# A layer on one core: where the shared expert's gate is applied, and when the expert slots are worked out and filled

## The reference, cut to what matters

```python
logits = x_flat @ gate_w.T                       # 8 experts, 512 tokens
scores = softmax(logits); w = scores * in_top2   # two experts per token
h = silu(g) * u                                  # routed experts, inner width 704
out = einsum('neh,ne->nh', expert_out, w)
shared = silu(x_flat @ shared_gate_w.T) * (x_flat @ shared_up_w.T) @ shared_down_w.T   # inner width 1408
shared_weight = sigmoid(x_flat @ shared_expert_gate_w.T)      # one number per token
out = out + shared_weight * shared
```

## Time and profile before

| | |
|---|---|
| median of three runs | 723.59 us |
| profiled execution, its time / its span | 723.02 / 721.3 us |
| PE busy | 699.9 us, 97% |
| DVE busy | 573.9 us, 80% |
| ACT busy | 336.3 us, 47% |
| POOL busy | 197.3 us, 27% |
| granted TensorE clock, mean | 0.995 |

### The profile page before, as it was taken

The page is one execution under the profiler, slowest core; times in us unless marked ns, Lnnn a source line. Parts: engine busy times, 40 slices in busy tenths (PEclk is TensorE's granted clock), DMA queues, the critical chain, the costliest instruction groups (busy, mean ns, idle before and its releaser), DMA issues.

```text
span 721.3 us, 9895 instructions
## 1 busy us (share of the span) xinstructions
PE 699.9 (97%) x3209; PEld 573.9 (80%) x3209; DVE 573.9 (80%) x714; ACT 336.3 (47%) x449; POOL 197.3 (27%) x143
## 2 busy tenths in 40 slices
PE   7999999999999999999999999899999999999996
PEld 6888888888887788888888888668777888888884
DVE  6477888777979998899994734678677799899896
ACT  4322222222245555656662424632233588887871
POOL 4335445454430000000000001334893111212153
PEclk9999999999999999999999999999999999999997
DMA  8046676776632237232202406122300799999973
GB/s 307 2 159 202 222 231 225 253 226 229 233 123 97 88 117 320 88 113 91 87 29 92 186 0 248 48 84 103 117 3 1 289 343 351 387 386 365 407 276 121
DMA packets 38541, 130.68 MB, mean 181 GB/s; under 512 B 6642, under 2 KB 10484, under 8 KB 35444
## 3 DMA queue, kind: packets, MB, share of 16 engines
q1 hardware_dynamic: 35972, 124.85, 47.8%
q0 software_dynamic: 1536, 4.20, 1.8%
q10 hardware_dynamic: 1008, 1.32, 0.6%
HBM read 120.89 MB, written 9.46 MB: 181 GB/s over the span
## 4 chain that ended last, share of the span: by engine, by line
PE 87%; DVE 9%; issue 2%; ACT 2%; DMA 0%; DVEq 0%; ACTq 0%
PE ps L886 21%; PE ps L853 8%; PE ps L849 8%; PE ps L850 8%; PE ps L1071 5%; PE ps L805 5%; PE ps L807 5%; PE ps L806 5%; PE ps L1041 4%; PE ps L1052 3%; PE ps L1050 3%; PE ps L1051 3%; DVE hid L1476 1%; PE ps L1058 1%; DVE wu_lo L1544 1%
## 5 line engine op out<-in xcount | busy, mean ns | idle before, releaser
L429 POOL TENSOR_TENSOR c_lo<-ring,c_hi 128x512 fp32r<-128x512 f32 x64 | 86.0, 1344 | 102.8 <-ACT c_hi L536 102.8
L434 POOL TENSOR_TENSOR w_lo<-raw,w_hi 128x1024 fp32r<-128x1024 f32 x11 | 26.8, 2434 | 270.8 <-ACT w_hi L663 270.7
L849 PE MATMUL ps<-qk_hi,c_hi 128*128 128x512 f32 x256 | 100.2, 391 | 0.1
L536 ACT ACTIVATE c_hi<-ring 128x512 fp32r<-128x512 f32 x64 | 40.4, 632 | 128.2 <-PE ps L853 96.1
L850 PE MATMUL ps<-qk_lo,c_hi 128*128 128x512 f32 x256 | 99.6, 389 | 0.0
L1235 DVE TENSOR_TENSOR runmax<-runmax,att 128x512 f32<-128x512 f32 x64 | 88.8, 1387 | 6.0 <-DVE att L1229 3.2
L1544 DVE TENSOR_TENSOR wu_lo<-raw_u,wu_hi 128x2048 fp32r<-128x2048 f32 (+1 forms) x33 | 69.9, 2119 | 12.8 <-ACT wu_hi L673 12.4
L1229 DVE SCALAR_TENSOR_TENSOR att<-ring,beta,ps 128x512 f32 (+1 forms) x64 | 47.8, 746 | 26.1 <-PE ps L853 25.5
L853 PE MATMUL ps<-qk_hi,c_lo 128*128 128x512 f32 x256 | 68.4, 389 | 0.0
L886 PE MATMUL ps<-p_hi,d_hi 128*128 128x512 f32 x256 | 64.2, 393 | 0.6 <-DVE ps L1312 0.6
L886 PE MATMUL ps<-p_hi,d_lo 128*128 128x512 f32 x256 | 63.2, 389 | 0.0
(11 more groups left out here) (299 smaller groups left out, 1502.1 us busy)
## 6 DMA issues: line engine op xcount, KB each, us to landing
ring<-stream SPq DMA_DIRECT2D x64, 512.0 KB, 4.2
raw_u<-up_in SPq DMA_DIRECT2D x22, 1024.0 KB, 7.2
raw_d<-down_in SPq DMA_DIRECT2D x33, 512.0 KB, 7.4
ring<-ctx_in SPq DMA_DIRECT2D x32, 512.0 KB, 3.2
raw<-shared_in SPq DMA_DIRECT2D x11, 768.0 KB, 4.6
raw_u<-up_last_in SPq DMA_DIRECT2D x11, 768.0 KB, 6.8
slots<-blank SPq DMA_DIRECT2D x15, 256.0 KB
late<-wqkv_in SPq DMA_DIRECT2D x1, 3072.0 KB, 10.0
```

Of the source, the lines that this page charges most:

```text
L429: pool.tensor_tensor(c_lo[:, s % 2, :], ring1[:, s, 0, :], c_hi[:, s % 2, :].bitcast(F32), ALU.subtract).then_inc(lo1_ready, 1)
L536: act.activation(c_hi[:, s % 2, :], ring1[:, s, 0, :], ACT.Copy).then_inc(hi1_ready, 1)
L849: pe.matmul(ps[:, s, :], hi, qk_hi[:, k, :], start=(k == 0), stop=False)
```

## The change

The gate is no longer multiplied into the hidden layer. gate_diag, its matmul, the tile wb and its semaphores are gone, and gate_col multiplies the finished sums as they are added into x. slot_rows stands behind hidden 1 and extra_units. POOL waits for rows_ready behind low_parts 3, scatters rows three, three and two at a time behind low_parts 3, 4 and 5, and pairs two at a time behind low_parts 6 to 9.

```diff
-            def scatter_rows(c):
-
-                for st in range(ST):
+            def scatter_rows(first, last):
+
+                for c, st in itertools.islice(itertools.product(range(2), range(ST)), first, last):
                     pool.indirect_dma_start(slots, bass.IndirectOffsetOnAxis(row_of[:, c, st:st + 1], 0),
                                             rows_n[:, st, :], None).then_inc(rows_out, 16)
...
             for n in range(1, SH):
                 low_parts(n, n % RAW, n % HL)
-                if n == 4:
+                if n == 3:
                     pool.wait_ge(cleared, 16 * (NU + 2))
                     pool.wait_ge(rows_ready, 1)
-                    scatter_rows(0)
+                    scatter_rows(0, 3)
+                if n == 4:
+                    scatter_rows(3, 6)
                 if n == 5:
-                    scatter_rows(1)
-                if n == 6:
-                    scatter_info(0)
-                if n == 7:
-                    scatter_info(1)
+                    scatter_rows(6, 8)
+                if 6 <= n < 10:
+                    scatter_info(2 * (n - 6), 2 * (n - 5))
...
-                if n == 0:
-                    act.wait_ge(wb_psum, 1)
-                    act.activation(wb[:, :], ps[:, 7, :], ACT.Copy).then_inc(wb_ready, 1)
...
-            def gate_and_counts():
-                pe.wait_ge(gate_ready, 1)
-                pe.matmul(ps[:, 7, :], ones[:, :], gate_diag[:, :, :].rearrange("p t c -> p (t c)"), start=True,
-                          stop=True).then_inc(wb_psum, 1)
+            def count_places():
                 pe.wait_ge(taken_ready, 1)
...
-            pe.wait_ge(wb_ready, 1)
             pe.wait_ge(counts_read, 1)
...
-            step(dve.reciprocal(gate_col[:, :], ex[:, :, E]))
-            dve.tensor_tensor(gate_diag[:, :, :], ident[:, :].unsqueeze(1).to_broadcast([P, ST, P]),
-                              gate_col[:, :].unsqueeze(2).to_broadcast([P, ST, P]), ALU.mult).then_inc(gate_ready, 1)
+            dve.reciprocal(gate_col[:, :], ex[:, :, E]).then_inc(gate_ready, 1)
...
                 dve.wait_ge(prod_done, n + (1 + CREDIT))
-                dve.wait_ge(wb_ready, 1)
-                step(dve.tensor_tensor(h, h, wb[:, :], ALU.mult))
                 dve.tensor_copy(h_hi[:, p, :], h).then_inc(hhi_ready, 1)
...
                     dve.wait_ge(down_done, SH + CREDIT)
+                    dve.wait_ge(gate_ready, 1)
                     for st in range(ST):
-                        dve.tensor_tensor(x[:, st, :], x[:, st, :], ps[:, 4 + st, :], ALU.add).then_inc(added, 1)
+                        dve.scalar_tensor_tensor(out=x[:, st, :], in0=ps[:, 4 + st, :], scalar=gate_col[:, st:st + 1],
+                                                 in1=x[:, st, :], op0=ALU.mult, op1=ALU.add).then_inc(added, 1)
...
                 if n == 1:
                     extra_units()
-                if n == 2:
                     slot_rows()
```

More of the change, by code:

```diff
@@ L1 @@
+import itertools
 from contextlib import ExitStack
@@ L165, in perceiver_layer @@
         y_lo = at("y_lo", [P, D], F32R, 170)
-        wb = at("wb", [P, S], F32, 172)
         xgn = at("xgn", [P, D], F32, 174)
@@ L208, in perceiver_layer @@
         info_s = at("info_s", [P, 2], F32, 151.8125)
-        gate_diag = at("gate_diag", [P, ST, P], F32, 202)
         gate_hi = at("gate_hi", [P, KC, E + 1], F32R, 200)
@@ L259, in perceiver_layer @@
         taken_ready, place_psum, gate_ready, counts_read = sem("taken_ready"), sem("place_psum"), sem("gate_ready"), sem("counts_read")
-        iota_ready, more_ready, wb_psum, wb_ready = sem("iota_ready"), sem("more_ready"), sem("wb_psum"), sem("wb_ready")
+        iota_ready, more_ready = sem("iota_ready"), sem("more_ready")
         cleared, rows_ready, xg_full = sem("cleared"), sem("rows_ready"), sem("xg_full")
@@ L447, in _, with scatter_info @@
                       allow_small_or_imprecise_dtypes=True).then_inc(iota_ready, 1)
-            def scatter_rows(c):
-                for st in range(ST):
+            def scatter_rows(first, last):
+                for c, st in itertools.islice(itertools.product(range(2), range(ST)), first, last):
                     pool.indirect_dma_start(slots, bass.IndirectOffsetOnAxis(row_of[:, c, st:st + 1], 0),
                                             rows_n[:, st, :], None).then_inc(rows_out, 16)
-            def scatter_info(c):
-                for st in range(ST):
+            def scatter_info(first, last):
+                for c, st in itertools.islice(itertools.product(range(2), range(ST)), first, last):
                     pool.indirect_dma_start(slot_info, bass.IndirectOffsetOnAxis(row_of[:, c, st:st + 1], 0),
@@ L1140, in _ @@
             up_shared(0, between=turn_logits)
-            up_shared(1, between=gate_and_counts)
-            pe.wait_ge(wb_ready, 1)
+            up_shared(1, between=count_places)
             pe.wait_ge(counts_read, 1)
```

## The result

The changed kernel takes 716.36 us (median of four executions, 716.15 to 716.92) where the kernel before takes 723.28 (four, 722.54 to 724.27): ratio 0.9893, interval 0.9869 to 0.9917. Forecast was a median of 718.0, range 716.5 to 720.8. The profiled execution took 716.92 us (span 715.2), 6.10 us less than the one before.

A forecast was written before the change was run, and what follows sets the result against it. PE was taken to set the time, so only its idle time and work could be won. 2.5 + 4.3 - 0.9 - 0.25 = 5.6 us takes the profiled 723.02 to 717.4, a median of 718.0 us, range 716.5 to 720.8.

The forecast's parts named there:

- What bounds, and the holes: Shared experts: PE sets the time, only its idle time and work can be won; 4.3 us lost after expert 3.
- the rival that its loads keep the gain: Routed experts: DMA at share 0.86 might set the pace, giving 723.6 us, no change; chance 0.05.
- Part 1: Up to expert 0's down projection: moving the gate to the sums starts it at 478.65 instead of 481.12, 2.5 us won.
- Part 2: Later shared experts: without the product with wb and with two or three scatters per expert, PE's holes go, 4.3 us won.
- down 7's hole: PE's 0.80 us wait for h_lo before expert 7's down projection, laid to the product with wb contending with POOL; would go.
- the three holes from groups of four: Smaller PE holes from three more groups of four scatters after up 5's, the rest of the 4.3 us; would go.
- Part 3: Expert 4's up projection: POOL waits earlier for the slots' rows, w_lo 4 comes late; 0.9 us lost (0.2 to 1.5).
- Part 4: The four adds: 0.74 us each instead of 0.68, with the next transposes waiting for them; 0.25 us lost.
- The sum: Whole kernel: 2.5 + 4.3 - 0.9 - 0.25 = 5.6 us won, a median of 718.0 us.
- no-stall case: Rival at up 4: DVE slips between POOL's subtractions, rows ready by 490.3; gain 6.5 us, 717.1 us; chance 0.12.
- The lock: DVE beside POOL: two-SBUF-tile instructions and POOL's SBUF reads exclude each other; trace agreed, but differed from the page's order.
- The prediction's case of the other order: Expert 4's product with wb started at 506.67, before POOL's subtraction at 506.98, and still took 4.51 us.

The follow-up runs named there:

- e2: Changed kernel with slot_rows back behind hidden 2 and scatters in fours behind low parts 4 to 7, so only the gate is moved; 715.80 us, ratio 0.9891.
- e5: Kernel of e2 with a product of hid with a tile of ones kept in every hidden(n); 720.23 us, ratio 0.9962 to the kernel before.
- e3: Kernel before, gate still in the hidden layer, with slot_rows behind extra_units and the changed kernel's scatters; 723.00 us, ratio 0.9989.
- e6: Kernel of e2 with the four adds plain as before and the gate left out altogether; 715.91 us, ratio 0.9900 to the kernel before.
- e8: Changed kernel with its scatters in fours behind low parts 3 to 6; 719.58 us, ratio 0.9963 to the kernel before.
- e7: Changed kernel with slot_rows back behind hidden 2, POOL's wait left behind low parts 3; 719.52 us, ratio 0.9947 to the kernel before.

## Why the prediction was right and wrong, step by step

- **What bounds, and the holes.** Right. PE sets the time, and all gains are its idle time and its own work. The routed stage is as long as before within its scatter; the rival that its loads keep the gain did not come.
- **Part 1, 2.5 us to down 0.** Measured 2.80 (17.51 to 14.71). The mechanism was right, the size 0.3 low. The cast was let in between POOL's two subtractions, and counts were read by 478.4, just as PE came: no wait at all, where I had left 0.15 us for one (478.65 against 478.5). The rest is that I took PE's 1.74 us of idle time as all that the hole cost, and it costs 0.2 more, as said of the other holes above.
- **Part 2, 4.3 us from the later experts.** The sum was nearly right (the products gone give 4.44: 78.34 to 73.90; 4.3 came from a step of 8.19 us, the mean of three of which the first, behind a hole, is 8.25, where 8.16 is the undisturbed one). The reason was not the one that acts here. The step of the mechanism that failed is "With two or three scatters per expert ... POOL ... does not fall behind. So down 7's hole and the three holes from groups of four go". With fours left in they go too (e2), and with the products put back in all return (e5). The smaller groups and the earlier rows also take these holes away, but alone they pay for it at up 4 (e3), and on top of the moved gate there is nothing left for them to gain. I compared POOL's work with PE's 8.19 us, and did not follow how early POOL starts. I had worked out hidden 1 as 0.7 us earlier for Part 3, and never asked what this does to the old order.
- **Part 3, 0.9 us lost.** Measured 0.49 (74.39 against 73.90). Rows ready at 490.89 for 491.2, first scatter 0.93 later for 0.94, three scatters 3.73 for 3.94, PE released at 498.06 for 498.6. The chain was right and each link a little shorter: 0.3 us of the 0.5 is the blocked DVE steps, 0.2 the scatters. It is the largest of the mis-sized terms. This is also all that the move of the slots brings here: a loss. On the kernel before it brings nothing that the medians tell (e3).
- **Part 4, 0.25 us lost.** Right up to the transposes of unit 1, then filled into a hole of 0.28 that was there (e6): 0.
- **The sum.** 2.80 + 4.44 - 0.49 = 6.75 us, for 5.6 forecast. The profiled execution shows 6.10: it reached the logits 0.22 later, and its routed stage took 0.4 more. The medians show 6.9, and 6.05 and 6.8 in the repeats. So what put the number off is four small terms of one sign: Part 3's loss 0.4 too large, Part 1's gain 0.3 too small, Part 4's loss 0.25 where there is none, Part 2's gain 0.14 too small. Another 0.3 is the kernel before itself, 723.59 from three executions and 723.28 from four. The range had at its lower end only the 0.6 us of scatter below a no-stall case of 717.1, which itself kept the 0.25. That the result lies 0.14 outside it and not inside is less than the 1.0 by which the kernel's own medians differ (716.36 to 717.34).
- **The lock.** The Trainium skill (SBUF — State Buffer, section Who interferes with whom) lets the one that issues first have the ports. In the changed kernel each of the three casts that was blocked started behind POOL's first subtraction, so these agree with it. The prediction's case of the other order, the product that started 0.31 us ahead of POOL's subtraction and was still held up, came again in e5 (504.96 for 4.50 us, POOL from 505.28), in both with a scatter of POOL ending between the two starts; the page's order does not give this, and nothing here explains it. That the cast of experts 3 and 4 stays out also at the boundary of the pair is not told there: it gets in where POOL's second subtraction had still to wait for ACT when the first began (expert 0), and not where both were ready (experts 4 and on). For this reading there are two cases of the first kind before (2.75 and 2.87 us, experts 0 and 2), one in e2 (row_of, 1.90), and several of the second; expert 3 of the changed kernel (3.60) is of the second kind as well. It was not tested by itself.

## What to carry to other kernels

An instruction on an engine that looks hidden can hold the path through a third one: count how much earlier its removal lets the next queue start, in every order, before crediting a second edit. When an edit has two parts, price each alone against the old order of the other; here one part was all of the gain, and the other, which had seemed needed for it, a small loss. A periodic producer that is slower than its consumer (8.62 to 8.16 us) is harmless for as many periods as its starting slack holds, so count that slack before making its bites smaller. Smaller bites help only where the slack is missing: fours in place of threes cost 3.3 us in the order of the changed kernel (e8) and nothing in the old one (e2).

## What the runs showed that I had not expected

- A PE hole of 2.09 us was followed by a granted clock of 0.62 over 4.5 us in one kernel (e3) and by 1.00 in another (e7), and one of 1.74 us in the kernel before by 1.00 (481.0 to 485.5). The fall cost 1.6 us beside the hole's own.
- An indirect DMA of POOL takes 0.96 to 0.99 us in most places. The first behind POOL's wait takes 1.17 to 1.19, 1.17 also in e7, where DVE is idle beside it, and 1.42 in the kernel before, where the cast h_hi falls into it. In e3 the third of a group is the long one, 499.74, with the cast at 500.18:

```profile
493.50 1.17 POOL L451 DMA_INDIRECT slots<-rows_n,row_of  x1 [7.30 <-DVE pairs L1528]
```
```profile
498.46 0.97 POOL L452 DMA_INDIRECT slots<-rows_n,row_of  x1 [0.30 <-issue]
499.74 1.25 POOL L452 DMA_INDIRECT slots<-rows_n,row_of  x1 [0.30 <-issue]
...
504.77 1.25 POOL L452 DMA_INDIRECT slots<-rows_n,row_of  x1 [0.16 <-issue]
```
```profile
500.18 0.43 DVE L1477 CAST h_hi<-hid 128x512 fp32r<-128x512 f32 x1
500.64 4.52 DVE L1479 TENSOR_TENSOR h_lo<-hid,h_hi 128x512 fp32r<-128x512 f32 x1
```

The first fence is e7, the others e3. The Trainium skill (SBUF — State Buffer, section SBUF: two separate sides) says that GpSimd cannot write descriptors while an fp32 copy of DVE from SBUF to SBUF holds the shared ports. The trace agrees at 499.74, by 0.27 us for a cast of 0.43. But the DMA at 504.77 is as long with no cast beside it, only the end of a subtraction h_lo that POOL's pair had held up. In the kernel before and in e5 the long scatter (1.25) meets both the end of such a product and the cast. That it is long is where POOL's 8.86 in place of 8.62 us per expert comes from; which of the two lengthens it was not tested.
